# A cross-attention and feed-forward kernel: first tile's column correction from PSUM, four-byte fillings, transposed integers of tiles 1 to 3 taken by VectorE

## What is computed

```
q1 = fake_quant(layernorm(x)); q2 = fake_quant(ctx)      # scale 8/255, zero point 128
x  = x + q1 @ q2
y  = layernorm(x)
g  = top-2 softmax of y @ gate_w.T over 8 experts
x  = x + y @ base_w.T + base_b + 2 * sum_e g_e * (y @ A_e.T) @ B_e.T      # rank 16
```

## Time and profile before

| | |
|---|---|
| median of 3 runs | 168.84 us (168.42 to 168.93) |
| the profiled execution, its own time | 169.07 us |
| its span, first to last instruction | 167.1 us |
| PE busy | 158.9 us, 95% of the span, 824 matmuls |
| DVE busy | 110.9 us, 66%, 250 instructions |
| ACT busy | 82.3 us, 49% |
| POOL busy | 35.0 us, 21% |
| granted TensorE clock | 1.00 |
| DMA | 32.68 MB, mean 196 GB/s |

### The profile page before, as it was taken

One profiled execution on the slowest core, in us unless ns is written; L12 is line 12 of the kernel. 1 busy time (PEld: TensorE's weight loads), 2 busy tenths in 40 slices (PEclk: granted clock), 3 DMA queues, 4 the chain that ended last, 5 costly groups with the idle time before them and its releaser, 6 DMA issues.

```text
span 167.1 us, 2359 instructions
## 1 busy us (share of the span) xinstructions
PE 158.9 (95%) x824; PEld 121.0 (72%) x824; DVE 110.9 (66%) x250; ACT 82.3 (49%) x107; POOL 35.0 (21%) x69
## 2 busy tenths in 40 slices
PE   5859998999999999999999999999999999999993
PEld 2224544788888768887868768878888888998882
DVE  6976688989989979999493927584750364322061
ACT  3089978872675556265357094446325544330000
POOL 3334026130731201403720520012071000000000
DMA  5999999949989999003995599951969993000024
GB/s 214 312 418 419 408 411 411 230 79 326 365 192 274 310 239 357 19 0 63 197 179 92 105 178 193 320 187 16 145 120 201 195 269 126 4 0 0 0 87 166
DMA packets 22045, 32.68 MB, mean 196 GB/s; under 512 B 13714, under 2 KB 13970, under 8 KB 22034
## 3 DMA queue, kind: packets, MB, share of 16 engines
q1 hardware_dynamic: 20016, 25.20, 46.9%
q0 software_dynamic: 2016, 7.34, 23.7%
q10 hardware_dynamic: 2, 0.00, 0.0%
HBM read 22.05 MB, written 4.19 MB: 157 GB/s over the span
## 4 chain that ended last, share of the span: by engine, by line
PE 82%; DVE 6%; DMA 4%; POOL 2%; ACT 2%; issue 1%; SPq 0%; DVEq 0%; ACTq 0%; POOLq 0%
PE ps_odd L1083 24%; PE ps_even L1083 20%; PE ps_att L1028 11%; PE ps_g L1064 5%; DMA x_sb<-in_ctx 4%; PE ps_t L1008 2%; PE ps_g L1067 2%; PE ps_even L1116 2%; PE ps_even L1118 2%; PE ps_even L1117 2%; PE ps_odd L1028 2%; PE ps_even L1036 2%; DVE x_sb L724 1%; POOL r_v L381 1%; PE ps_odd L1145 1%
## 5 line engine op out<-in xcount | busy, mean ns | idle before, releaser
L1083 PE MATMUL ps_odd<-w_hi,yt 128*128 128x512 f32 x128 | 38.4, 407 | 0.0
L1028 PE MATMUL ps_att<-c,c1t 128*128 128x512 f16 x96 | 31.4, 383 | 0.0
L1083 PE MATMUL ps_even<-w_hi,yt 128*128 128x512 f32 x96 | 27.7, 401 | 0.0
L1083 PEld LDWEIGHTS ps_odd<-w_hi,yt 128*128 128x128 f32 x128 | 23.7, 189 | 5.0 <-issue 0.2
L1064 PE MATMUL ps_g<-ag,yt 128*128 128x272 f32 x64 | 21.2, 375 | 0.0
L1083 PEld LDWEIGHTS ps_even<-w_hi,yt 128*128 128x128 f32 x96 | 17.9, 188 | 3.6
L1083 PE MATMUL ps_odd<-w_lo,yt 128*128 128x512 f32 x64 | 20.0, 401 | 0.0
L518 ACT ACTIVATE y_words<-yt_planes 128x1024 uint16<-128x1024 uint16 x8 | 10.3, 1353 | 14.1 <-DMA yt_planes<-y_planes 14.1
L1083 PE MATMUL ps_even<-w_lo,yt 128*128 128x512 f32 x48 | 15.1, 406 | 0.0
L718 DVE SCALAR_TENSOR_TENSOR x_sb<-ps_att,q_ss,x_sb 128x512 f32<-128x512 f32 x12 | 8.4, 746 | 9.6 <-PE ps_att L1028 6.6
L445 ACT ACTIVATE qc<-ring,q_in,q_rec 128x1024 uint16<-128x1024 f32 x11 | 13.3, 1231 | 1.6 <-issue 1.6
(11 more groups left out here) (142 smaller groups left out, 297.0 us busy)
## 6 DMA issues: line engine op xcount, KB each, us to landing
ring<-in_ctx SPq DMA_DIRECT2D x12, 512.0 KB, 7.4
x_sb<-in_x SPq DMA_DIRECT2D x8, 512.0 KB, 8.3
w_raw<-in_w_t SPq DMA_DIRECT2D x8, 512.0 KB, 11.4
x_sb<-in_base_b POOLq DMA_DIRECT2D x8, 512.0 KB, 8.1
out_x<-x_sb SPq DMA_DIRECT2D x15, 256.0 KB, 2.4
x_sb<-zfix POOLq DMA_DIRECT2D x6, 512.0 KB, 6.8
x_sb<-in_ctx SPq DMA_DIRECT2D x4, 512.0 KB, 7.6
ag_raw<-in_ag_t SPq DMA_DIRECT2D x1, 544.0 KB, 13.1
```

Source lines behind the costliest of these rows:

```text
L1028: ins = pe.matmul(att_bank(t)[h][:, :], c1t[:, t % 4, k, :], c2[:, k, h * HALF:(h + 1) * HALF], start=(k == 0), stop=(k == CT - 1))
L1083: pe.matmul(ffn_bank[t % 2][h][:, :], rows_of(part, t, k), w[:, k, h * HALF:(h + 1) * HALF], start=start, stop=False)
```

## The change

Three edits of operations, and new orders on all five engines.

The fillings write the same bytes as four-byte elements, half as many, and those of tiles 1 to 3 move in DVE's list from the start to behind quantise_first, cut_context(2) and scale_context(5). take_c1t leaves ACT for DVE. Tile 0 gets its column correction on DVE straight from PSUM (add_columns: x += ps_even * ssd1, half by half, before its attention is added; the constant ssdd goes into rowfix of tile 0), and add_zfix on DVE is left for tile 1 alone. ACT's zero_point_columns(0) reads the second bank first, and the first one only after DVE has read it. attention(2, 0, h) waits for both readers. variance(1, 0) no longer waits for an addition of zfix.

```
+TWO_ONES = struct.unpack("<f", struct.pack("<HH", 0x6400, 0x6400))[0]
...
             def byte_ones(t):
-                dve.memset(c1[:, t, :], BYTE_ONE).then_inc(bytes_ready, 1)
+                dve.memset(c1[:, t, :].bitcast(F32), TWO_ONES).then_inc(bytes_ready, 1)
...
+            def take_c1t(t):
+                dve.wait_ge(c1t_psum, t + 2)
+                dve.tensor_scalar(c1t[:, t].rearrange("p k m -> p (k m)"), ps_th,
+                                  -(BYTE_ONE + CENTRE), 1.0, ALU.add, ALU.mult).then_inc(c1t_ready, 1)
...
             def add_attention(t):
                 if t == 0:
-                    dve.wait_ge(ss_ready, 1)
+                    dve.wait_ge(columns_taken, 2)
...
+            def add_columns():
+                dve.wait_ge(colsum_psum, 1)
+                dve.wait_ge(ss_ready, 1)
+                dve.wait_ge(qx_ready[0], 2)
+                for h in range(2):
+                    if h == 1:
+                        dve.wait_ge(zfix_ready, 1)
+                    cols = slice(h * HALF, (h + 1) * HALF)
+                    dve.scalar_tensor_tensor(out=x_sb[:, 0, cols], in0=ps_even[h][:, :], scalar=ssd1,
+                                             in1=x_sb[:, 0, cols], op0=ALU.mult, op1=ALU.add).then_inc(columns_taken, 1)
...
-                for h in range(2):
+                for h in (1, 0) if b == 0 else (0, 1):
+                    if b == 0 and h == 0:
+                        act.wait_ge(columns_taken, 1)
...
                     if t == 2:
-                        pe.wait_ge(zfix_ready, 2)
+                        pe.wait_ge(columns_taken, h + 1)
+                        pe.wait_ge(zfix_ready, 2 - h)
```

More of the change, by code:

```diff
@@ L312, in _ @@
             transpose_c1(4)
-            for k in range(11, 16):
+            for k in range(13, 16):
                 load_context(k)
+            store(0, 0)
             load_x(6)
+            store(0, 1)
             load_x(7)
+            store(1, 0)
+            store(1, 1)
             transpose_c1(5)
@@ L825, in _ @@
             row_of_ones()
[L826 to L827 removed]
+            byte_ones(0)
             take_scales()
[L829 removed]
             quant_reciprocals()
@@ L870, in _ @@
+            x_shift(4)
+            weigh_low(0)
             split_w_lo(2)
[L871 to L879 removed]
             cut_context(8)
             cut_context(9)
+            cut_x(4)
+            split_w_lo(3)
+            normalise_x1(2)
+            split_w_lo(4)
+            cut_context(10)
@@ L882, in _ @@
             top_logits(1)
-            split_w_lo(6)
-            split_w_lo(7)
+            add_attention(3)
+            for k in range(5, 8):
+                split_w_lo(k)
             split_b_lo()
             split_low_lo(0)
-            cut_context(10)
+            cut_context(11)
             weigh_low(1)
-            cut_context(11)
+            finish_tile(0)
+            split_y_lo(2, 0)
             cut_context(12)
-            split_y_lo(2, 0)
-            finish_tile(0)
-            cut_context(13)
@@ L1310, in _ @@
             base(2, 6)
-            for k in range(0, 4):
-                base(3, k)
             transpose_y(3, 1)
+            attention(4, 7, 1)
+            base(3, 0)
+            base(2, 7)
+            base(3, 1)
+            base(3, 2)
             attention(5, 0, 0)
+            attention(5, 0, 1)
             transpose_low(2)
-            attention(5, 0, 1)
             attention(5, 1, 0)
@@ L1403, in _ @@
             low_and_gate(5, 7)
-            for k in range(0, 4):
-                base(5, k)
+            base(4, 6)
+            base(5, 0)
+            base(4, 7)
+            base(5, 1)
+            lora(4, 0)
+            base(5, 2)
+            base(5, 3)
             transpose_low(5)
-            base(4, 6)
-            base(4, 7)
-            lora(4, 0)
             lora(4, 1)
@@ L1455, in _ @@
             lora_last(0)
-            base_last(1, 7)
             lora_last(1)
-            for k in range(4, 8):
+            for k in range(3, 8):
                 base_last(2, k)
```

473 lines of the change are left out of this document (238 added, 235 removed).

## The result

The changed kernel is slower. Its five runs gave a median of 172.08 us (169.54 to 174.54) against 168.84 for the kernel before; the ratio, which leaves out its two slowest runs (174.54 and 172.69, the profiled one), is 1.0101 (95% interval 1.0053 to 1.0149). So it lost 1 to 2% (1.0% by the ratio, 1.9% by the medians) and gained a scatter that the kernel before doesn't have. The forecast was 168.2, and its range ended at 169.2. The profiled execution took 172.69 us (span 170.8), 3.6 more than that of before (169.07).

What follows compares the result with a forecast made beforehand. TensorE was taken as the bound from 9.9 us on, so only its waits before 38 us could go. 169.07 - 0.8 + 0.15 = 168.4 us, against the median 168.2; range 167.5 to 169.2.

Steps and rivals of the forecast that it cites:

- The head: Start to the last column sums: earlier fillings and transposes, a new 0.8 us wait, in sum 0.2 us gained.
- Case A: Tile 0's second statistics: POOL's root starts before DVE's subtraction, y near 27.55, total 168.2 us; chance 0.47.
- rival 1: POOL's root is held by DVE's subtraction, y of tile 0 near 28.1; 168.65 us, no change; chance 0.28.
- The gain: Tile 1's transposes at 36.2 instead of 37.02, waiting for the zfix DMA: 0.8 us, the head's 0.2 included.
- rivals 3 and 4: Four-byte filling takes 1.07 us: 168.9, chance 0.06; the 0.8 us wait before attention(1, 0, 0) doesn't arise: 167.4, chance 0.07.
- Costed at nothing: Takes for tiles 2 and 3, row sums, weight splits, moved stores and later stages: no cost beneath a full TensorE.
- tight places: base(2, 0), attention(5, 0, 0), base_last(1, 0): under 0.2 us TensorE slack; none over 0.3, together 0.15 (0 to 0.6).
- sign of being wrong: Tile 1's transposes after 37.0, half speed in TensorE's warming, or half a microsecond's wait at a tight place.
- rival 2: add_attention(4) on DVE becomes the bound and delays attention(5, 0, 0) by 1.3 us: 169.5 us; chance 0.12.
- given back: Later TensorE waits at three places with under 0.2 us of slack: 0.15 us, between 0 and 0.6.
- half-speed stretch: TensorE's warming running at half speed, listed among what would show the forecast wrong; no size given.

Runs made afterwards that it cites:

- c1: Changed kernel with one POOL wait: base_b loads into tiles 2 and 1 go out only after c1(4)'s DMA transpose has landed; 169.11 us, ratio 1.0001.
- a3: Changed kernel with ScalarE's split_low_hi(0) ahead of scale_context(13) and split_y_hi(2, 0) ahead of scale_context(14); 169.2 us, ratio 1.0015.
- a2: Changed kernel without the loads that add base_b to tiles 0 to 2 or the waits for them (output incomplete); 168.42 us, ratio 0.9985.
- a0: Changed kernel timed again, unedited; 171.52 us, ratio 1.0093.
- a1: Changed kernel with w tiles 6 and 7 loaded before context tiles 10 and 11 on SyncE; 169.97 us, ratio 1.0065.
- e2: Changed kernel with a3's ScalarE order, c1's POOL wait and load_x(5) behind transpose_c1(4); 168.48 us, ratio 0.999.
- d3: d1 without keep_warm(), the three matmuls between the two halves of the first transposes; 169.71 us, ratio 1.0063.
- c3: Changed kernel with all orders of a4, c1's POOL wait and six added warm matmuls in the head; 168.99 us, ratio 1.0015.
- e3: c3 with load_x(5) behind transpose_c1(4), and three warm matmuls behind attention(0, 0, 0) in place of its six; 168.43 us, ratio 0.9985.
- a4: Changed kernel with the order edits of a1 and a3, and scale_context(10) behind split_w_hi(7); 169.03 us, ratio 1.0022.
- d1: c3 without its six warm matmuls, and with add_bias(0) ahead of x_scale(4) and rstd_x1(2) on POOL; 169.69 us, ratio 1.0051.
- c2: Changed kernel with only six warm matmuls added in the head, every order left; 171.19 us, ratio 1.006.

## Why the prediction was wrong

**The head was right.** The filling took 0.48 us (0.53 forecast). The first transposes came at 7.89 (8.1), the wait before attention(1, 0, 0) was 0.66 us (0.8), column sums 7 at 20.30 (20.6), tile 0's mean was there at 25.51 (25.8). Four DVE rows of after:

```profile
8.34 0.48 DVE L680 MEMSET c<- 128x512 f32 x1
...
20.99 1.51 DVE L742 SCALAR_TENSOR_TENSOR x_sb<-ps_even,q_ss,x_sb 128x512 f32<-128x512 f32 x2
...
27.18 0.81 DVE L763 TENSOR_SCALAR y<-x_sb,mv,rstd 128x1024 f32<-128x1024 f32 x1
...
34.12 1.41 DVE L730 SCALAR_TENSOR_TENSOR x_sb<-ps_even,q_ss,x_sb 128x512 f32<-128x512 f32 x2 [0.83 <-DMA x_sb<-zfix]
```

The filling's value isn't zero and its time still halves, which goes beyond the zeros of which the Trainium skill, "VectorE: DVE Perf Modes", section on zero memsets, speaks.

**Case A held against rival 1.** POOL's root began at 25.87 and DVE's two-input subtraction at 25.98, and the root took 0.55 us:

```profile
25.60 0.19 POOL L387 TENSOR_SCALAR r_v<-mv 128x1 f32<-128x1 f32 x1 [3.46 <-DVE mv L670]
25.87 0.55 POOL L388 TENSOR_TENSOR rstd<-r_v,minus_half 128x1 f32<-128x1 f32 x1
26.43 2.56 POOL L400 DMA_DIRECT2D x_sb<-zfix  x2
```

**Tile 1's transposes came at 36.39 (36.2), 0.63 earlier than before.** The gain was forecast as 0.8. Most of what is missing is the zfix transfer: issued 1.6 us earlier, it took 7.7 us, not 6.3, so that the y behind it waited as forecast but longer. Up to here the sum was good to 0.2 us, and rivals 3 and 4 fell with it. Part of that is luck. The forecast moved the issue of the zfix transfer by what it moved y of tile 0, to about 27.6, and left it 6.3 us; it was issued at 26.43, right behind the root, and took 7.7. The two errors, 1.2 and 1.4 us, cancel. Smaller ones: y of tile 0 began at 27.18, not 27.55, and the take of a whole tile cost 0.64 us, below the lower bound of 0.68 (whose 256 ns stand for 256 steps, 0.27 us at the forecast's own pace).

**The step that failed is "Costed at nothing".** I let the row sums, splits and moved transfers go "by microseconds, under a TensorE that is full", and looked for tight places only in the lists of DVE and POOL. I priced none of four things: w tiles 6 and 7 behind two contexts, whose landing add_bias(0) waits for and which the prediction doesn't mention at all; normalise_x1(2) forward, which sends add_bias(2) and (1) out 3.7 us earlier, at 49.90; three context loads issued in the same microseconds, whose landings this doubled (11.3 against 5.6 us, shown by c1); and ScalarE's list, in which scale_context(13) and (14) stand directly ahead of what TensorE needs (shown by a3). The loss needs them together: taking away the loads (a2), delaying two of them (c1) or changing ScalarE's order (a3) gives back 2.3 to 3.1 us of a0's median, and brings the ratio from 1.0093 to 0.9985, 1.0001 and 1.0015. With the w tiles first alone (a1) it is 1.5 us and 1.0065. None of the moves was tried alone in the kernel before.

One of my three tight places was in fact hit, which I had named as a sign of being wrong, but not for my reason. The wait of 1.34 us at 66.27 is base(2, 0) behind split_y_lo(2, 0), to which I gave no more than 0.3. I had feared finish_tile(0) ahead of it on DVE; that ended at 64.5, and DVE then stood 0.95 us for ScalarE's half, which was queued behind scale_context(14):

```profile
63.08 1.40 DVE L845 SCALAR_TENSOR_TENSOR x_sb<-ps_odd,rowfix,x_sb 128x512 f32<-128x512 f32 x2
65.43 0.69 DVE L769 TENSOR_TENSOR yt<-ps_t,yt 128x512 fp32r<-128x512 f32 x1 [0.95 <-ACT yt L541]
```

The other two lost nothing: after 70 us TensorE was full, at attention(5, 0, 0), rival 2's place, too. The outcome was slower, and for none of my reasons.

**Where the 3.7 us between the spans lie.** e2's TensorE works off the same list as the changed kernel's and doesn't stop after 38 us, so matmul can be held against matmul:

```profile
36.00 0.60 PE L1038 MATMUL ps_t<-ident_f,y 128*128 128x128 f32 x4
...
53.44 0.39 PE L1059 MATMUL ps_att<-c,c1t 128*128 128x512 f16 x1
...
58.77 0.39 PE L1175 MATMUL ps_odd<-b_hi,lt_hi 128*128 128x512 f32 x1
...
61.91 0.70 PE L1114 MATMUL ps_odd<-w_hi,yt 128*128 128x512 f32 x2
...
163.34 0.28 PE L1156 MATMUL ps_att<-b_hi,lt_lo 128*128 128x256 f32 x1
```

The changed kernel lies 0.39 us behind e2 at tile 1's transposes (36.39), then 1.32, 2.80 and 4.36 behind the three stops. So they cost 0.93, 1.48 and 1.56 us, 3.97 together, and not their idle time of 3.4, since in a full stretch a matmul starts before the one ahead has ended. The rest is the new order itself. From tile 1's transposes to the last matmul e2 takes 127.34 us and the kernel before 127.00 (37.02 to 164.02), without a wait in either; two gate matmuls more and one of attention less lie in between now, which about cancel (0.24 and 0.22 us). That is 0.34 given back where I had put 0.15. Together: -0.63 + 3.97 + 0.34 = 3.7 us, which is the difference of the spans, 170.8 and 167.1.

**The mechanism forecast is there once that is mended.** In e2's profile tile 1's transposes come 1.02 us earlier than before and the last matmul 0.68 (163.34 against 164.02). In the times this isn't shown: e2 and e3, with medians of 168.48 and 168.43 and best runs at 168.04 and 167.96, are near the 168.2 that I gave the change, but the 0.3 us by which they lie below the kernel before is less than what a measurement here can tell from no change.

**What stays open.** First, what brings the falls of the clock. Executions with a mean clock of 0.99 or less were 14 of 116 with the changed head and no added warm matmuls (times 169.7 to 178.6), 1 of 56 with some, the one after the stop at 54 us, and none of 137 of the kernel before. The one fall in the head that a profile caught is in a3: behind a wait of 0.77 us the matmuls, otherwise 0.22 us apart, stand 0.43 apart until 15.7, and TensorE is 1.6 us later from there on than in e2.

```profile
11.23 0.38 PE L1057 MATMUL ps_att<-c,c1t 128*128 128x512 f16 x1
12.38 0.50 PE L1057 MATMUL ps_odd<-c,c1t 128*128 128x512 f16 x1 [0.77 <-DVE c1t L696]
12.67 0.63 PE L1057 MATMUL ps_att<-c,c1t 128*128 128x512 f16 x1
13.10 0.63 PE L1057 MATMUL ps_odd<-c,c1t 128*128 128x512 f16 x1
```

The counts speak for the idle pieces of the pulled-forward head, but the kernel before is idle longer there (busy 1.99 of 4.00 us from 8 to 12, a3 2.58) and d3 widened a piece without a fall in its six runs. The forecast had named a half-speed stretch as a sign of being wrong and given it no price. What stands here is a correlation, not a cause. Second, what of the traffic slows the DMA transpose. Fewer loads around it help: a2 has 3.5 us, and c3 and e3, in which it and the load into tile 0 go out at nearly the same times (47.02 and 44.30, 47.17 and 44.35) and which differ in load_x(5) and three warm matmuls, have 6.8 and 4.8. The share of each load wasn't separated. Third, why a1's contexts landed early beside the two loads and a4's, with these at 49.25, did not. No profile caught one of the runs of 176 to 179 us.

## What to carry over

A list of work in order is also a list of waits: when a change moves loads or their waits, write down for each engine's list which item waits for a transfer, and what stands behind it that the bounding engine needs, directly or through a third engine (d1: POOL's load, DVE's shift, TensorE); then ask what else is issued in the same ten microseconds. A load that became ready earlier isn't free, it takes the landing time of those issued beside it. And an operation that reads a shared bank early (here the correction from PSUM) pays only where its place in the list is early too; try it without the new orders, and the orders without it.

## What I hadn't expected of the hardware

- Three 512 KB context loads, issued from 49.3 to 53.3 us, landed after 10.4 to 12.2 us with two accumulating loads issued through the other queue at 49.90, and after 5.5 to 6.4 us with these at 54.84 (the changed kernel and c1). In a1, with them at 51.00, 0.74 us behind the first context, it was 4.9 to 8.7.
- The DMA transpose of one tile took 3.2, 3.5, 4.2, 4.8, 5.5, 6.5, 6.9 and 7.7 us in different kernels: with the exception of the last it landed between 52 and 55 us, whether it was issued at 47.2 (e3) or at 49.4 (d1).
- After a stop of 1.9 us in the middle of a full stretch (c2) TensorE's granted clock was 0.67 of the full one on average from 56 to 60 us: part of them was spent at 1.2 GHz instead of 2.4. After the stops of 1.3 us in the changed kernel it stayed at 1.00.
